# Four attention layers on one core: weights in four transfers, the set-up's products in two PSUM banks, and new tables of turns

## What is computed

```python
def _L0(x, ctx, ctxb, ...):
    xn, kv = layernorm(x), layernorm(ctx)
    x = x + mha(xn, kv, W_qkv, W_o)                    # 8 heads of 32
    U = (layernorm(x) @ W_in.T + b_in) @ Bmat
    def step(s, u_t):
        s = silu(s @ A.T) + u_t
        return (s, s)
    states = scan(step, 0, U)                          # 1024 steps
    x = x + states @ Cmat
    return x + (ctxb.mean(axis=1) @ W_prog.T + b_prog)[:, None, :]
x = _L0(x, ctx, ctxb, ...)
x = x + causal_attention(layernorm(x), layernorm(ctx), wq, wkv, wo)     # L1, 16 heads of 64
x = layernorm(x + masked_attention(x, ctx, Wq, Wk, Wv, Wo))             # L2, 16 heads of 16
x = x + masked_attention(layernorm(x), layernorm(ctx), q_w, kv_w, proj) # L3, 16 heads of 16
x = x + gelu(layernorm(x) @ fc1 + b1) @ fc2 + b2
```

## Time and profile before

| | us |
|---|---|
| median of 3 runs | 1443.99 |
| lowest and highest | 1443.29, 1445.27 |
| the profiled execution's own time | 1445.13 |
| its span, first to last instruction | 1443.4 |
| outside the span | 1.7 |
| PE busy | 1362.1 (94%) |
| DVE, ACT, POOL busy | 935.7, 675.1, 559.2 |

### The profile page before, as it was taken

One profiled execution on the slowest core, in us unless ns is written; L12 is line 12 of the kernel. 1 busy time (PEld: TensorE's weight loads), 2 busy tenths in 40 slices (PEclk: granted clock), 3 DMA queues, 4 the chain that ended last, 5 costly groups with the idle time before them and its releaser, 6 DMA issues.

```text
span 1443.4 us, 22984 instructions
## 1 busy us (share of the span) xinstructions
PE 1362.1 (94%) x8763; PEld 1130.9 (78%) x8763; DVE 935.7 (65%) x2204; ACT 675.1 (47%) x1497; POOL 559.2 (39%) x700
## 2 busy tenths in 40 slices
PE   6999999999899989999999999989998999899989
PEld 4887886767688768878887887868876887698768
DVE  3677764487755776586768466785677567746771
ACT  2566655423455343534454535345434644454344
POOL 4345332013732363345244411283147215620661
PEclk8999999999999999999999999999999999999999
DMA  5043412020000000000000001000000000000000
GB/s 142 23 91 109 137 52 77 1 68 1 1 8 16 8 1 15 9 8 5 5 9 1 23 1 17 16 1 9 22 1 1 9 23 1 0 9 1 1 0 23
DMA packets 46730, 34.10 MB, mean 24 GB/s; under 512 B 21980, under 2 KB 45339, under 8 KB 46107
## 3 DMA queue, kind: packets, MB, share of 16 engines
q1 hardware_dynamic: 45287, 32.43, 8.0%
q10 hardware_dynamic: 1332, 0.17, 0.1%
HBM read 23.26 MB, written 8.39 MB: 22 GB/s over the span
## 4 chain that ended last, share of the span: by engine, by line
PE 75%; DVE 13%; POOL 4%; ACT 4%; issue 2%; DMA 1%; ACTq 1%; DVEq 0%
PE ps L871 9%; PE ps L831 9%; PE ps L881 9%; PE ps L927 8%; PE ps L938 7%; PE ps L850 7%; PE ps L841 5%; PE ps L891 5%; PE ps L797 5%; PE ps L780 4%; DVE zt L1321 3%; PE ps L1032 2%; DVE mx L1346 2%; DVE stat L1308 1%; PE ps L1045 1%
## 5 line engine op out<-in xcount | busy, mean ns | idle before, releaser
L1577 POOL TENSOR_TENSOR rstd<-mv,halfneg 128x1 f32<-128x1 f32 x192 | 109.4, 571 | 490.6 <-DVE mv L1312 489.4
L1158 ACT ACTIVATE pr<-pr 128x616 f32<-128x616 f32 x224 | 159.8, 715 | 177.2 <-DVE pr L1351 89.3
L1616 POOL TENSOR_TENSOR pr<-mx,pr 128x616 f32<-128x616 f32 x128 | 156.5, 1224 | 212.4 <-DVE mx L1346 211.0
L1162 ACT ACTIVATE pr<-ps 128x512 f32<-128x512 f32 x224 | 132.1, 597 | 148.6 <-PE ps L850 148.4
L850 PE MATMUL ps<-ident,pr 128*128 128x128 f32 (+1 forms) x1120 | 160.9, 277 | 8.5 <-POOL pr L1602 4.9
L1410 DVE TENSOR_TENSOR xt<-xt,ps 128x256 f32<-128x256 f32 x192 | 80.0, 416 | 130.6 <-PE ps L891 68.3
L881 PEld LDWEIGHTS ps<-vtab,pr 128*128 128x128 f32 (+1 forms) x1280 | 153.5, 192 | 12.9 <-ACT pr L1162 8.6
L881 PE MATMUL ps<-vtab,pr 128*128 128x102 f32 (+1 forms) x1280 | 161.3, 274 | 1.2 <-ACT pr L1162 1.0
L850 PEld LDWEIGHTS ps<-ident,pr 128*128 128x128 f32 (+1 forms) x1120 | 124.9, 139 | 35.1 <-POOL pr L1602 14.8
L871 PE MATMUL ps<-vwo,pr 128*128 128x256 f32 (+1 forms) x640 | 148.9, 382 | 0.1
L831 PE MATMUL ps<-wk,tt 128*128 128x308 f32 x512 | 145.9, 427 | 1.5 <-DVE xt L1410 1.0
(11 more groups left out here) (200 smaller groups left out, 2414.9 us busy)
## 6 DMA issues: line engine op xcount, KB each, us to landing
out_dram<-xt SPq DMA_DIRECT2D x64, 128.0 KB, 1.7
xt<-in_x_dram SPq DMA_DIRECT2D x32, 128.0 KB, 2.5
xt<-out_dram SPq DMA_DIRECT2D x32, 128.0 KB, 2.1
fc<-in_L_xattn_fc_w_dram SPq DMA_DIRECT2D x2, 1024.0 KB, 5.4
wk<-in_L_xattn_wkv_dram SPq DMA_DIRECT2D x1, 2048.0 KB, 8.1
front<-in_L_xattn_wkv_dram SPq DMA_DIRECT2D x1, 2048.0 KB, 7.7
wo<-in_L_xattn_wo_dram SPq DMA_DIRECT2D x1, 1024.0 KB, 5.4
kb<-in_L_xattn_wq_dram SPq DMA_DIRECT2D x1, 1024.0 KB, 6.6
```

The costliest lines, as they stand in the source:

```text
L1158: ac(v, v, ACT.Exp, scale=-ATTN[key[0]].scale).then_inc(done["expo"], 1)
L1162: ac(pr[:, run.lane, 0:4 * P], bank(run.lane, 0), ACT.Copy).then_inc(done["pturn_main"], 1)
L1577: p.tensor_tensor(rstd[:, n:n + 1], mv[:, n, 1:2], halfneg[:, :], ALU.pow).then_inc(done["rstd"], 1)
L1616: p.tensor_tensor(p8, mx[:, run.lane, :].unsqueeze(2).to_broadcast([P, HG, KEYS]), p8, ALU.subtract).then_inc(done["below"], 1)
```

## The change

**Four transfers.** `WKV_PARTS = 4`: each `wkv1_get` becomes four, each with a quarter of the 2048 columns, and `k_mm` waits for all four. Each has its own place in SP's string.

**Two banks for the set-up.** `ITEM_BANKS` is now `(6, 7)`, the banks of lane 3. Product n waits until product n-2 is emptied, no longer n-4. Lanes 0, 1 and 2 no longer wait for the set-up as a whole; they still wait for what they read.

**New turns.** All five strings of `TURNS` are new. The steps and their count are the same, but for six more transfers on SP.

```diff
+WKV_PARTS = 4
...
-    steps = [] if pair else ([("v0_put", p)] + [("weights_get", i) for i in range(LOADS - 1)] + [("wkv1_get", p), ("masks", "2"), ("weights_get", LOADS - 1)])
+    wkv1 = [("wkv1_get", p + str(i)) for i in range(WKV_PARTS)]
+    steps = [] if pair else ([("v0_put", p)] + [("weights_get", i) for i in range(LOADS - 1)] + wkv1 + [("masks", "2"), ("weights_get", LOADS - 1)])
...
-        steps += [("wkv1_get", p)]
+        steps += wkv1
...
-ITEM_BANKS = (4, 5, 6, 7)
+ITEM_BANKS = (6, 7)
...
-        "iiiiiiiiiiii1i0iiiiiiii0iiii0ii123120203102301021310123020110323103102102020121330031021302112310212320310321021"
+        "iiiiiii1i0iii10iii2i10ii21ii0ii0i1ii2i01ii0310230310210231031213023022013010233102031301201132102102302103202303"
...
-                sp.dma_start(wkv1[int(key)], by_rows("L1_xattn_wkv")).then_inc(wkv1_in, 16)
+                pair, part = map(int, key)
+                n = 2 * L1.width // WKV_PARTS
+                cols = slice(part * n, (part + 1) * n)
+                sp.dma_start(wkv1[pair][:, :, cols], by_rows("L1_xattn_wkv")[:, :, cols]).then_inc(wkv1_in, 16)
...
-                        pe.wait_ge(wkv1_in, 16 * (pair + 1))
+                        pe.wait_ge(wkv1_in, 16 * WKV_PARTS * (pair + 1))
```

More of the change, by code:

```diff
@@ new lines @@
+    "scalar": (
+        "iiiiiii0i1021i1ii0i0i21ii0ii123032103003121103021013220231303020123101103210213022023010323321030121130131202322"
+        "0100323321031211032102322130210200313302031311203212201302002133302130321113202213013233210300231013112032122313"
+        "302132323100123aa23saasasasasasasaassaasaasaasaasaaaasaaasaasaasasaasssssssssssssss01023102132031020130211023201"
+        "2133020130121320023110303212010202313102010233121013302103120120130130123102011320301032123002123003231120301120"
+        "3212013001323210110233120311230201213003121032201333210232031032121302203131320021313002210132130020321112032031"
+        "03132120320130103221210310323102032103132120031212030131230203103121203203103212bb1323bbbbbb2332bb2bb323bbbb2302"
+        "2031031302102321030312023121023131230203103121203023031102211323020130132201003231132100232103123210231030103212"
+        "0312023112330201301321200321310301212030320121331020210312310320212302133102301230301220132102313123020310312120"
+        "3023101302121003230121313020201331210203221301332102023103013212031023121303202301312102302331010221313020231310"
+        "2120303032131213322"),
@@ new lines @@
+    "gpsimd": (
+        "ii102i2i3i130010001112232302303001111220202303a31301a12012020320331311122220303031013121220230303101312212203303"
+        "3011012232333120123301a2b011023320100121220301313200020101131302222112033323102033110322101332120001130013100000"
+        "2011121213031322100323222210333103321321302001213132032011300001110112230213302213302220211230233033132132201300"
+        "1132003312100001111100122203313220313021222233332332320023113230320012112020331312000203013110122212333123203132"
+        "0311002231123033200011212203013132000201113130022121232330321330211300213320123230001121230203131200020311131002"
+        "22122133303213302130102211332203300101102023231310002020313110122212333130223312031132230"),
@@ L666, in wkv1_get @@
             def wkv1_get(key, run):
-                if key == "0":
+                pair, part = map(int, key)
+                n = 2 * L1.width // WKV_PARTS
+                cols = slice(part * n, (part + 1) * n)
+                if pair == 0:
                     sp.wait_ge(set_mm, len(ITEMS))
```

86 lines of the change are left out of this document (35 added, 51 removed).

## The result

| | before | changed |
|---|---|---|
| median, us | 1443.64 | 1381.63 |
| lowest and highest, us | 1442.16, 1445.27 | 1378.09, 1385.81 |
| runs | 4 | 4 |
| profiled execution, us (its span) | 1445.13 (1443.4) | 1379.43 (1377.7) |

The ratio is 0.957, with a 95% interval from 0.956 to 0.959. The direction was right, and so was the mechanism of the set-up. What I had set to nothing, "all other turns", holds nearly all of the gain.

The account below looks back on a forecast made before the run. It took PE as the bound: its work, idle time and low-clock loss make the span. Terms 4.0 + 3.6 + 0.7 = 8.3 us took 1445.1 to 1436.8, forecast as a median of 1435.7 us, range 1428.5 to 1442.

Parts of the forecast that it names:

- Term 4, all other turns: Rest of phase one and phase two: neighbours change places throughout; taken as 0, with ends of 3 us on both sides.
- No edit changes PE's work: Whole kernel: the span is PE's work, 1362.1 of 1443.4 us busy, plus its idle time and low-clock loss.
- term 2: Phase one: weights in four transfers free a late load of x; 1.93 us of waits and 1.7 of clock, 3.6 together.
- term 3: Recurrence: 0.9 us charged at its start, 1.6 won at its end; 0.7 us, ends -1 and 2.
- No group of waits stands out: PE's idle 11.2 + 49.4 us in the rest of phase one and phase two shows no outstanding waits; 0 taken.
- Term 1, the set-up: Set-up: hole of 3.3 us instead of 5.3; 0.65 us idle plus 3.4 clock, 4.0 won, ends 0.65 and 7.4.
- The clock doesn't fall: Rival, set-up: clock stays up after the hole, so 7.4 us are won there: 1432.3 us; chance 0.14.
- The quarters don't help: Rival, phase one: four pieces leave the load of x late, so their gain is 0: 1439.3 us; chance 0.08.
- The two banks become the bound: Rival, set-up: thirteen products each wait 1.1 us for a copy, 14.3 us new idle: 1450.0 us; chance 0.06.
- The last of my signs for a wrong forecast: Behind 304 us: PE's idle time changed by more than 3 us, which the prediction does not see at all.

Follow-up runs that it names:

- pe_drain: Changed kernel with a wait added on PE, ahead of 185 turns of phase two, for PE's own preceding step: 1418.15 us.
- p2_new: Kernel before with only the phase-two turns of the changed kernel, four banks and one transfer kept: 1408.04 us, ratio 0.976.
- p2_old: Changed kernel with the phase-two turns of the kernel before, all else as changed: 1420.65 us, ratio 0.984 to before.
- swap_calm: Kernel before with 62 exchanges of neighbours in PE's turns at random places where neither step waited: 1496.03 us, ratio 1.037.
- swap_few: Kernel before with 12 exchanges of neighbours in PE's turns, at the 12 largest waits such an exchange can cover: 1449.82 us, ratio 1.0045.
- setup_new: Kernel before with the changed kernel's set-up turns and two banks, later turns and the one transfer as before: 1439.93 us median of ten, ratio 0.997.
- quarters: Kernel before with each pair's weights in four transfers in place of one, turns otherwise and four banks as before: 1446.45 us, ratio 1.0013.
- whole_after: Changed kernel with each pair's weights in one transfer again, in place of the first quarter: 1379.28 us, ratio 0.957 to before.
- banks_two: Kernel before, old turns, with the set-up's products on two banks in place of four: 1446.46 us, ratio 1.0017.
- yield_before: Kernel before, turns unchanged, with POOL waiting for the norm its rstd releases before another lane's prebias, keep, below or maskmul: 1443.21 us, ratio 1.000.

## Why the prediction was wrong

**"No edit changes PE's work", so the span is work, idle time and clock.** This step failed first. The busy time of the page isn't the work: it holds a part of the waits. In phase two the 23.3 us of idle time that went took 12.5 us of busy time with them, 10.8 without the clock, and waits as short as those of `pe_drain` show a quarter of their cost as idle. My account of 81 us that could be won was short from the start; by the records' distances there were 166 or more.

**Term 4, all other turns: 0, with ends of 3 us.** This step made the miss. By `p2_new` and `p2_old` phase two is worth 36 us, and phase one with the recurrence 20.5 by the comparison at equal clock, of which I had the waits of term 2 and the 0.7 of term 3. I had seen that neighbours change places by two to four steps throughout, and that "nothing in the trace shows what one such exchange does". From that I took nothing, as if an exchange cost nothing. `swap_calm` says that one in PE's string alone costs 0.84 us on average, at places that look idle-free. So tables that differ in hundreds of places may differ by tens of us, and the ends of term 4 should have been tens of us, not 3. "No group of waits stands out" was true and beside the point: `swap_few` shows that covering the waits that stand out wins nothing (6.1 us slower, 2.2 without the clock). The sign could have been had from the two orders. In POOL's order alone, 104 of the 192 `rstd` have such a step of another lane right behind them before and 61 in the new one (76 and 24 of these start at once in the traces), and a sign of the price stood in the trace of before: 70 norms of over twice their length.

**Term 1, the set-up: 4.0, ends 0.65 and 7.4.** The mechanism held, with the DMAs on ACT 1.2 to 1.4 us later than counted (23.42 to 28.80 for 22.2 to 27.4): the hole 3.33, the clock back before 36 us, the scores before 26. `setup_new` has a median 4.0 below that of before. That the median agrees is luck, since it stands for 2.8 in seven runs and 10.2 in three, and 10.2 is above my upper end. The loss at low clock, which I took as 3.4 us, one number between 1.7 and 6.8 (3.4 to 13.6 us at half clock), lies at either end in this set-up, 1.7 or 6.9. In the seven the clock wins nothing then (6.9 by `p2_old`'s profile against 6.8 before), and the 2.8 us are idle time and order, where I had 0.65.

**Term 2, the quarters: 3.6.** The waits and the low clock between 165 and 190 us did go, but not by the quarters: `quarters` is 1.8 slower and `whole_after` loses nothing. The failed step is that I counted the new place among the loads and credited the size. The rule of the Trainium skill that I had weighed against it (DMA: Bandwidth & Descriptors, "Rules for kernel authors": join small transfers) agrees with `quarters`, for 2 MB and 512 KB; in `whole_after` the joined transfer is neither better nor worse.

**Term 3, the recurrence: 0.7, ends -1 and 2.** It was 2.3 us (61.40 to 59.10). The wait at the first `ssm` shrank by 0.7, from 1.82 to 1.16, not to 0.2:

```profile
272.16 0.67 PE L924 MATMUL ps<-cmat,scan 128*128 128x256 f32 x2 [1.16 <-ACTq L1254]
```

The rest came from the start and from between, which I had charged with 0.9: PE idles 1.8 us in the whole recurrence, where it was 4.1.

**The rivals.** "The clock doesn't fall" happened in one profile, that of the changed kernel without `prebias`, and in none of those with the full program. "The quarters don't help" did. "The two banks become the bound" has its price: 1.8 us by `banks_two`, not 14.3 (which had counted thirteen products from `wprog` on; `ITEMS` has 27 in all, not 30, and ten of them from there). None of them could have reached 1381.6, since all moved the same small terms. The last of my signs for a wrong forecast, PE's idle time behind 304 us changed by more than 3 us, is the one that came: 23.7 us, from 49.9 behind the first `ssm` (49.4 from 304 us on the earlier trace rows) to 26.1.

**What stays open.** The runs show that the gain is made by the turns of phase one and phase two, that it is spread over more than a hundred waits, and that the large waits can't be taken out by exchanges in PE's string alone. Why the new order has fewer waits stays open. The clash of norm and POOL is one cause, with 3 to 6 us for `prebias`; its whole share, between 8 and 21 of the 62 us, is worked out, not shown, and the rest has no named cause. Which engine's string brings how much wasn't tried.

## What to carry to other kernels

Where an engine is 94% busy through an order made by hand or by search, don't size a new order by the shown idle time or by its largest waits; compare each step's distance to the next with the tightest one of its kind, since that holds what a wait hides in "busy". Give a table that moves everywhere ends of tens of us, and look in the two orders for what can be counted, here which step stands right behind one that releases another engine. Before crediting an edit that came with a new order, ask what it does in the old one: here both the banks and the transfers made that slower, by 1.8 us each. And compare runs at equal mean clock before you explain a few us.

## What the runs showed of the hardware

A `norm` on DVE (float32, SBUF to SBUF, one source) that starts just after POOL has begun an addition, subtraction or multiplication ends only with POOL's instruction: 0.41 us becomes up to 1.47. Of the 77 norms of the kernel before that start while such an instruction runs, 73 end 0.13 to 0.17 us behind it. With POOL held back, all 192 took 0.36 to 0.51. Other operations of DVE kept their times beside the same instructions, also where they read SBUF: the maximum over 616 columns there took 791 ns while POOL worked and 786 without. The Trainium skill says as much (SBUF — State Buffer, "SBUF: two separate sides": the pair of ports that DVE and GpSimd share is locked for a whole instruction by the one that starts first, and the other engine waits; for DVE this holds in a two-port mode or with two SBUF inputs); the trace agrees, with 73 of those 77 norms. That the norm runs in a two-port mode is not shown by any run here.

A wait of PE for its own last product costs 0.20 us (36.1 to 36.7 us for 185), and three quarters of that are counted as busy time (27.1 of 36.7).

After a hole of 3.2 to 3.5 us of PE in the set-up the granted clock fell to 0.50, the level of 1.2 GHz, in the profiles of the changed kernel, `setup_new` and `p2_old`; it lost 1.7 us in the first two and 6.9 in the last, whose set-up is the same step for step. The ten runs of `setup_new` fall into the same two kinds. In the profile without `prebias` it did not fall at all after a hole of 3.15 us. After the hole of 5.3 us it lost 6.8, 8.5 in the profiles of `yield_before` and `swap_few`, which keep that set-up, and no run of the kernel before had the higher mean clock.
